# Two weighted direct rows of a sparse graph attention: added by TensorE in PSUM instead of by VectorE

## The reference

```
q, k, v = x @ Wq.T, x @ Wk.T, x @ Wv.T
scores = where(adj.T, q @ k.T, -1e30)
attn = where(adj.T, softmax(scores, axis=1), 0)
x = layernorm(x + attn @ v)          # twice, with weights of its own each time
```

## Time and profile before

| | |
|---|---|
| median of three runs | 204.85 us (200.79 to 205.75) |
| profiled execution, its time | 201.88 us |
| its span, first to last instruction | 200.1 us |
| mean granted clock of TensorE | 0.91 |
| busy: PE, DVE, ACT, POOL | 158.3, 123.5, 98.2, 144.3 us |

### The profile page before, as it was taken

The page is one execution under the profiler, slowest core; times in us unless marked ns, Lnnn a source line. Parts: engine busy times, 40 slices in busy tenths (PEclk is TensorE's granted clock), DMA queues, the critical chain, the costliest instruction groups (busy, mean ns, idle before and its releaser), DMA issues. The chain is left out here.

```text
span 200.1 us, 3716 instructions
## 1 busy us (share of the span) xinstructions
PE 158.3 (79%) x1068; PEld 134.3 (67%) x1068; DVE 123.5 (62%) x586; ACT 98.2 (49%) x285; POOL 144.3 (72%) x223
## 2 busy tenths in 40 slices
PE   2698999799999798396756887998687789877940
PEld 0586988689998687296644566897566578756730
DVE  1359688476777685868843032673838474857842
ACT  2003615676366672835772123762619274645870
POOL 5089698999899899899000899988899989998000
PEclk9999978999999999759978559999999957996998
DMA  6999993311334353435213133332234353434213
GB/s 181 297 322 301 345 310 92 84 47 52 85 103 112 100 148 92 132 94 141 79 56 105 52 90 88 88 79 79 80 97 143 79 138 93 141 84 132 74 52 113
DMA packets 20998, 24.91 MB, mean 124 GB/s; under 512 B 2032, under 2 KB 17904, under 8 KB 20976
## 3 DMA queue, kind: packets, MB, share of 16 engines
q0 software_dynamic: 4608, 12.59, 23.3%
q1 hardware_dynamic: 16368, 12.06, 20.3%
HBM read 20.45 MB, written 4.19 MB: 123 GB/s over the span
## 5 line engine op out<-in xcount | busy, mean ns | idle before, releaser
L792 DVE CUSTOM_DVE_ANT_0 prod<-Q,xd,d_none 128x256 f32<-128x256 f32 x64 | 30.2, 489 | 17.2 <-DMA xd<-x_rows,d_row 12.6
L352 POOL DMA_INDIRECT xd<-in_x,d_row x32 | 31.9, 995 | 12.1 <-DVE d_row L668 7.0
L1051 PE MATMUL PS<-M,xt 128*128 128x256 f32 x128 | 36.0, 430 | 3.7 <-ACT xt L444 3.7
L1167 PE MATMUL PS<-WvT,y_sb 128*128 128x256 f32 x128 | 36.0, 405 | 1.9 <-ACT y_sb L518 1.9
L347 POOL MEMSET pause<- 128x320 bf16 (+1 forms) x92 | 36.0, 392 | 0.1
L352 POOL DMA_INDIRECT xd<-x_rows,d_row x32 | 32.2, 1006 | 5.3 <-issue 5.3
L1051 PEld LDWEIGHTS PS<-M,xt 128*128 128x128 f32 x128 | 25.9, 213 | 8.0 <-ACT xt L444 4.6
L357 POOL DMA_INDIRECT xo<-x_rows,e_row x16 | 16.1, 1005 | 17.5 <-DMA x_rows<-X 15.0
L1167 PEld LDWEIGHTS PS<-WvT,y_sb 128*128 128x128 f32 x128 | 22.6, 196 | 5.8 <-ACT y_sb L518 2.8
L1155 PE MATMUL PS<-ident,both_rows 128*128 128x128 f32 x64 | 19.7, 308 | 8.5 <-DVE both_rows L833 6.2
L1157 PE MATMUL PS<-weight,xo 128*128 128x128 f32 x128 | 25.9, 304 | 0.0
(11 more groups left out here) (120 smaller groups left out, 282.5 us busy)
## 6 DMA issues: line engine op xcount, KB each, us to landing
adj_words<-in_adj SPq DMA_DIRECT2D x4, 1024.0 KB, 9.8
x_rows<-X SPq DMA_DIRECT2D x7, 256.0 KB, 2.1
out<-X SPq DMA_DIRECT2D x7, 256.0 KB
X<-in_x SPq DMA_DIRECT2D x2, 512.0 KB, 9.1
X<-in_x SPq DMA_DIRECT2D x1, 1024.0 KB, 10.1
W<-in_L_gnn_Wq SPq DMA_DIRECT2D x2, 256.0 KB, 6.6
W<-in_L_gnn_Wk SPq DMA_DIRECT2D x2, 256.0 KB, 6.8
xd<-in_x,d_row POOLq DMA_INDIRECT x32, 3.1
```

Source lines behind the costliest of these rows:

```text
L352: pool.indirect_dma_start(xd[:, t, k, :], None, rows, bass.IndirectOffsetOnAxis(ap=d_row[:, t, k:k + 1], axis=0)).then_inc(d_in[t][k], 16)
L792: dve.tensor_tensor_reduce(out=prod[:, S * j + k, :], in0=Q[:, t, :], in1=xd[:, t, k, :], op0=ALU.mult, op1=ALU.add, scale=-1.0, scalar=d_ ...
L1051: last = nc.tensor.matmul(PS[:, 7, j * D:j * D + D], xt[:, z % 2, j, h, :], M[:, z // PAIRS, h, :], start=(h == 0), stop=(h == H - 1))
L1167: last = nc.tensor.matmul(projected_into(j), y_sb[:, n % 2, j, h, :], WvT[:, layer, h, :], start=(h == 0), stop=(h == H - 1))
```

## The change

ScalarE multiplies both direct rows by their exponents into `direct_part`. VectorE's `both` is taken out. TensorE transposes the first part as before and adds the second with a plain matmul against the identity, into the same place of PSUM, and then adds the overflow part. ScalarE's exponents no longer wait for `both_in`; the new function waits for `y_ready` of two pairs before instead, since `direct_part` is read by TensorE.

```diff
-            def first_rows(layer, p, a, b):
+            def direct_parts(layer, p, a, b):
 
                 n = layer * PAIRS + p
                 act.wait_ge(s["totalled"], 2 * n + b)
+                need(act, "y_ready", 2 * (n - 1))
                 for j in range(a, b):
-                    act.activation(first_row[:, n % 2, j, :], xd[:, 2 * p + j, 0, :], ACT.Copy,
-                                   scale=exps[:, n % 2, j, 0:1]).then_inc(s["first_in"], 1)
+                    for k in range(S):
+                        act.activation(direct_part[:, n % 2, j, k, :], xd[:, 2 * p + j, k, :], ACT.Copy,
+                                       scale=exps[:, n % 2, j, k:k + 1]).then_inc(s["parts_in"], 1)
...
-            def both(layer, p, j):
-
-                n = layer * PAIRS + p
-                need(dve, "y_ready", 2 * (n - 1))
-                dve.wait_ge(s["first_in"], 2 * n + j + 1)
-                dve.scalar_tensor_tensor(out=both_rows[:, n % 2, j, :], in0=xd[:, 2 * p + j, 1, :], scalar=exps[:, n % 2, j, 1:2],
-                                         in1=first_row[:, n % 2, j, :], op0=ALU.mult, op1=ALU.add).then_inc(s["both_in"], 1)
...
-                pe.wait_ge(s["both_in"], 2 * n + j + 1)
+                pe.wait_ge(s["parts_in"], S * (2 * n + j + 1))
                 pe.wait_ge(s["a_ready"], 2 * n + j + 1)
                 y = summed_at(j)
                 for h in range(H):
-                    nc.tensor.matmul(y[:, h * P:h * P + P], both_rows[:, n % 2, j, h * P:h * P + P], ident[:, :],
-                                     is_transpose=True, start=True, stop=False)
+                    at_d = slice(h * P, h * P + P)
+                    nc.tensor.matmul(y[:, at_d], direct_part[:, n % 2, j, 0, at_d], ident[:, :], is_transpose=True, start=True,
+                                     stop=False)
+                    nc.tensor.matmul(y[:, at_d], direct_part[:, n % 2, j, 1, at_d], ident[:, :], start=False, stop=False)
                     last = nc.tensor.matmul(y[:, h * P:h * P + P], xo[:, t, h * P:h * P + P], weight[:, n % 2, j, :],
                                             start=False, stop=True)
```

More of the change, by code:

```diff
@@ L143, in edges_and_dense @@
         prob = sb("prob", [P, 2, 2])
-        first_row = sb("first_row", [P, 2, 2, D])
-        both_rows = sb("both_rows", [P, 2, 2, D])
+        direct_part = sb("direct_part", [P, 2, 2, S, D])
         y_sb = sb("y_sb", [P, 2, 2, H, P])
@@ L174, in edges_and_dense @@
             dist_ready own_ready own_t_ps own_t_sb l_ps listed over_ready flag m_ps m_sb xt_ps xt_sb q_ps q_sb
-            rested qe_ready e_done s_done sk_in sk_ready masked topped me_ready ds_ready totalled first_in both_in p_ready a_ready
+            rested qe_ready e_done s_done sk_in sk_ready masked topped me_ready ds_ready totalled parts_in p_ready a_ready
             y_ready y_sb_ready o_ready res stats spread logged rooted scaled normed normed_last x1_stored stored""".split()
@@ L486, in exponents @@
                 act.wait_ge(s["topped"], 2 * n + b)
-                need(act, "both_in", 2 * (n - 1))
                 for j in range(a, b):
@@ L556, in _ @@
                     exponents(layer, p, a, b)
-                    first_rows(layer, p, a, b)
+                    direct_parts(layer, p, a, b)
                     overflow_weights(layer, p, a, b)
@@ L575, in _ @@
                 exponents(layer, p, 1, 2)
-                first_rows(layer, p, 1, 2)
+                direct_parts(layer, p, 1, 2)
                 overflow_weights(layer, p, 1, 2)
@@ L914, in _ @@
                     inverses(layer, p, 0, 2)
-                    both(layer, p, 0)
-                    both(layer, p, 1)
                     if layer == 0 and p == 5:
```

## The result

The changed kernel takes **213.93 us** (median of 4 runs, 212.06 to 215.54) against 203.34 us for the kernel before (4 runs): a ratio of **1.058, 95% interval 1.047 to 1.069**. It is slower by 10.6 us. In a second measurement, on another chip and beside other runs, the ratio was 1.063 (1.054 to 1.073). The prediction was 213 us in 205.5 to 218.5, slower. The profiled execution took 215.54 us, with a span of 213.7; it is the slowest of the four, 1.6% above the fastest (212.06), so that differences taken from its profile are larger than the 10.6 us of the medians.

A forecast was written before the change was run, and what follows sets the result against it. Gathers were taken to bound layer 1's middle, a chain over engines both layers' ends. Layer 0's 6.5 us plus the tail's 3.4 made 9.9: 211.8 from the profiled execution, 214.8 from the median; stated 213, range 205.5 to 218.5.

The forecast's parts named there:

- The bound and the chain: Gathers pace layer 1's middle, so added work is free there; the ends of both layers follow a chain over engines.
- TensorE: In the sums: 64 more plain matmuls, 4 a pair, 0.88 us a pair at full clock, 1.76 at half.
- ScalarE: Two more copies a pair ahead of the overflow weights: tops to sums grows from 2.50 to 3.32 us in pair 6.
- VectorE: Its sum, 32 times 487 ns, goes; relief counted as 0, with 0.1 us remaining in the last tile.
- Pair by pair: Layer 0's lateness after slack: 3.4 us before pair 3, 4.4 before pair 5, 6.5 at the layer's end.
- The clock: Layer 0, pair 5's sums and an expansion: shorter idle time keeps the clock up and gives back 2.2 us.
- The tail: End of layer 1: 2.5 us before pair 7's slots plus 0.44 each for tiles 14 and 15, 3.4 us.
- The sum: Whole kernel: 6.5 us from layer 0 plus 3.4 from layer 1's tail, 9.9 us; 211.8 from the profiled execution.
- (a): Clock stays up in the chain's three half-clock stretches: 6.5 us more, 208 to 211; chance 0.20.
- (b): Clock falls in more places, pair 5 of layer 0 and pair 4 of layer 1: up to 14 us, 216 to 219; chance 0.17.
- (c): Sums wait for VectorE's sum, so ScalarE's extra work is hidden: 2.5 to 4.6 us, 204 to 209; chance 0.13.
- (d): Faster, if VectorE's 15 us set the pace; chance 0.04.

The follow-up runs named there:

- the second execution: Another profiled execution of the changed kernel; 79.2 us from pair 0's tops to layer 1's first gather, against 80.8 in the first.
- ScalarE's other order: Tile 0's ScalarE instructions, weight included, before tile 1's: on the changed kernel 207.64 us, ratio 1.031; on the kernel before 204.89 us.
- putting the load back: Changed kernel plus a VectorE multiplication and addition per tile, of the old size and place, result unread: 216.23 us, ratio 1.060.
- TensorE's part: Kernel before, with VectorE only weighting the second direct row and TensorE adding it by plain matmul: 205.58 us, ratio 1.013.
- ScalarE's part alone: Changed kernel without the second plain matmul, so the second direct row is left out of the sums: median 207.07 us, no interval.

## Why the prediction was right

**The bound and the chain.** That layer 1's middle is free and layer 0 isn't held: 68.68 us lie between the first gather of layer 1 and pair 6's tops after, 68.65 before. The lateness gathered in layer 0 and in the tail, as said; in the second execution nearly all of it in layer 0.

**TensorE.** 0.22 us for one added matmul, by starts, and 64 more of them. As counted.

**ScalarE.** 3.32 us predicted from tops to sums in pair 6, 3.30 measured. That the weight comes last although the waits named VectorE's sum was right. In the kernel before with ScalarE's other order, the weight comes 0.4 us earlier and the way falls by 0.38 us, to 2.12; and the whole 0.8 us of the two copies appears in the changed kernel. The other order there brings back 6 us.

**VectorE.** Counted at 0; putting the load back changed nothing that can be measured. In layer 1's last tile 2.51 us lie between tops and sums after and 2.26 before, so 0.25 remained there and not 0.1.

**Pair by pair.** Predicted lateness of tops 3.4 before pair 3 and 4.4 before pair 5; measured 4.2 and 5.2, of which 0.5 is the later start.

**The clock, the step that failed.** "If the clock then stays up ... I take the first, since the idle time halves": it fell, halfway into pair 5's sums, and again in pair 6's. Pair 6's tops were 6.4 us late instead of 3.9, tile 15's 10.8, and the first gather 11.1 us instead of 6.5, each with 0.5 of a later start in it. I had added up the pauses; but the pause just before the sums grew, from 2.28 to 2.98 us before pair 5 and from 1.56 to 2.37 before pair 6. Filled with idle products, the same kernel has its gather at 116.37, and layer 0 is 5.4 us shorter. So the layer's loss was 4.1 us larger than the term in this execution, and 2.5 in the second. Of the 4.1, some 0.3 had come up before pair 5's tops, 1.7 in pair 5, where the relief of 2.2 us was counted, 0.7 in pair 6 and 1.4 in pair 7.

That filling the pauses keeps the clock up in layer 0 is shown: behind pair 5's tops it was 1.00 up to pair 7 in all six profiles with idle products. What exactly lets it fall is not. Behind the pause of 2.98 us it fell in all five profiles that have it, and behind 2.36 to 2.37 in all four; behind 1.57 before pair 6's sums it fell in the change with the other order and not in TensorE's part, and behind 1.59 us before the sums of layer 1's pair 6 it fell in two of four profiles, of the changed kernel itself once in two.

**The tail.** 3.4 predicted, 2.5 measured in the first execution and 0.5 in the second, where the clock stayed at 1.00 from pair 6's tops to 200 us; the prediction's own value for a tail at full clock was 1.3. In the first, from pair 6's tops to tile 14's it is 7.71 us instead of 5.76, so 1.95 more and not 2.5, as the first of its sums still ran at full clock. Tile 14's 0.44 us wasn't on the path at all: 4.82 us lie between the tops of tiles 14 and 15 in both kernels.

**The sum** came out at 9.9 us against 10.6 between the medians and 13.7 between the two profiled executions. It was near the measurement in part by luck: a term too small for layer 0 met one too large for the tail, and the stated 213 stood above the sum's 211.8. The mechanism was right, the clock's term too small. (A slip in the chances: the forecast, (a) and (b) add up to 0.83, not 0.82.)

**The rivals.** (a), a clock that stays up, is what TensorE's part does alone in layer 0: 1.00 from 82 to 105 us. In the whole change it fell there; that ScalarE's copies undid it fits the longer pauses but isn't shown apart from them. (b), more half clock, is nearer to what happened in layer 0. (c), copies that are hidden, is refuted by the 3.30 us from tops to sums, in the changed kernel and in ScalarE's part alone, and by the order (6 us). (d) is refuted by the slower result itself, and the load put back shows VectorE off the path. Whether plain matmuls count for the clock where transposes don't, as the Trainium skill, page "TensorE: Matmul & The Clock Gate", Part 4: PE-mode transpose, has it, no run separates: TensorE's part added time and plain matmuls at once.

**What the change is made of**, each with an uncertainty of about a point. With idle products in all: TensorE's matmuls 3.4 points (0.979 to 1.013), ScalarE's copies in the better order none (1.014), the order as the change has it 1.5 (1.029). Idle products give the kernel before 2.1 points (6 in a pause) and the change about 3 (8 in a pause), so the clock accounts for about one point of the difference, and TensorE's matmuls for the largest part. The shares depend on what is taken first: without idle products TensorE's part is 1.3 points and what ScalarE adds to it some 4.5.

## What to carry to other kernels

Moving a sum from one engine to two others counts where the path is: here VectorE's 15 us were off it, and ScalarE's 0.8 us a pair were on it, ahead of an instruction that the same consumer also waited for. Before adding work in front of a shared wait, see which of the awaited is last by its end in the timeline, not by the name in the list of waits, and put what the first consumer needs first. Where a chain has pauses of TensorE of two to three microseconds, look at the granted clock behind each of them: an idle product there may be worth more than the change under study.

## What the runs showed that I had not expected

- The clock can fall inside dense work: from 91.7 us TensorE was busy without a gap and ran at 0.50 for 3.2 us, after a pause of 2.98 us that ended at 90.66.
- The clock is not the same from one execution to the next: in the two profiles of the changed kernel the tail's sums ran at 0.52 (193.9 to 197.2 us) in one and at 1.00 in the other, with the same pause of 1.59 us before them, and the tails differ by 2.0 us.
- A part of a change seems to pay in clock for what it costs in instructions: TensorE's part alone 1.3 points over the kernel before, but 3.4 where both have idle products.
- A multiplication alone on VectorE was on average no faster than the multiplication and addition that it stood for: 510 ns against 487. Single ones took 333 to 922 ns, against 471 to 668; what stretched the long ones is open.

```profile
L834 DVE TENSOR_SCALAR second_row<-xd,exps 128x256 f32<-128x256 f32 x32 | 15.2, 510 | 0.0
```
